# Projections as three one-pass products from stored high and low parts, and four maximum units moved between score blocks

## The chip, the cores and the metric

The kernel runs on one core of a Trainium2 chip. The metric is device time in microseconds (us) of one launch. The engines are TensorE (PE: matrix products; PEld: its weight loads), VectorE (DVE), ScalarE (ACT), GpSimd (POOL) and SyncE (SP), which here issues all transfers.

## The reference

Input x is 2 batches of 2048 rows of 256 numbers, float32. Attention with 16 heads of 64 runs on the normalised rows; then three blocks of a quantised two-layer network with low-rank terms follow.

```
keys    = einsum('bse,neh->bsnh', residual, W_key) + Bias_key      # queries, values alike
scores  = einsum('bknh,bqnh->bnqk', keys, queries) / sqrt(64)
scores  = where(q < k, 1e-10, scores)          # masked keys keep a weight
probs   = softmax(scores)
out     = einsum('bnqk,bknh->bqnh', probs, values) -> W_output + Bias_output
x = x + attention(layernorm(x));  x = x + ffn(layernorm(x))
```

The masked scores are not minus infinity, so every query also takes the sum of the values of all later keys, times exp(-maximum). The kernel therefore needs each row's maximum before its scores.

## The kernel before

Attention works on **pairs** of heads (8 per batch, 16 in all) and on **chunks** of 512 queries, taken in the order 3, 2, 1, 0. A pair has 20 **tiles** of four key blocks each; a tile is one turn of TensorE's loop: the two score blocks of the next tile (`scores`, n = 0 and 1), then the two halves of this tile's product with the values (`weighted`). While pair i does this, the preparation of pair i+1 is spread over it by tables of **slots**, six to a tile: slots 6t and 6t+1 come after the first score block, 6t+2 and 6t+3 after the second, 6t+4 and 6t+5 after each half of `weighted`. `between` issues what a slot holds.

Prepared in slots are:

- twelve **projection units** (`project`, slots 3, 5, 9, 11, ... 35): query, key and value of a chunk, each a 128x256 by 256x512 product in float32 from the normalised, turned x, which stays in SBUF (`xs`, a view of `home`). ScalarE rounds the result to the high part (`high`, L933) and copies that to bf16; VectorE takes the low part (`low`, L1071); a value unit has only VectorE's copy (L1066);
- forty **maximum units** (`max_unit`, table `MAX_AT`): for each head a bf16 product of 128 queries with up to 512 keys, whose maximum VectorE reads (`take_max`, L1085 and L1088);
- turned values, turned maxima and sums of probabilities (table `FIN`).

All of these write three background banks of PSUM in strict rotation: a projection takes one bank, a maximum unit two, one for each head. `bank_read` makes TensorE wait until the user three banks back has been read, so what sets the order around the change is these tables together with the rotation.

Scores are sums of one-pass products of high and low parts (float32r), 64 rows for each head, the heads side by side in the array; GpSimd adds up the probabilities (L669, L676), 18 of the 20 tiles of a pair. A row's maximum goes over DRAM to a row of SBUF (`keep_max`, `install_max`). SyncE issues everything in one written order and blocks on each wait. The second batch's x is normalised and turned while pair 6 runs. In the last pair VectorE does GpSimd's additions; then the weights of the network are turned, and the network runs as a block of its own.

Of the kernel before, what the change touches and what calls it, by code (L numbers as in the profile page):

```python
# [7 lines left out]
F32 = mybir.dt.float32  # L8
# [7 lines left out]
P = 128  # L16
CH = 512
# [70 lines left out]
PROJ_CHUNKS = [3, 2, 1, 0]  # L88
PROJ_SLOT = [6 * (u // 2) + (3, 5)[u % 2] for u in range(NPROJ)]
MAX_AT = [11, 15, 17, 21, 23, 27, 29, 33, 35, 37, 39, 41, 45, 47, 49, 51, 53, 57, 59, 61, 63, 65, 69, 71,  # L90
# [55 lines left out]
STATS_AT = {3: 50, 2: 56, 1: 78, 0: 84}  # L146
RSTD_TILE = {3: 10, 2: 11, 1: 14, 0: 15}
XN_AT = {3: 67, 2: 73, 1: 93, 0: 99}
TURN_AT = {3: 76, 2: 82, 1: 102, 0: 108}
# [43 lines left out]
def attention(nc, x, w_qkv, b_qkv, ffn_weights, max_kept, kept, inverses, ot, home):  # L193
# [14 lines left out]
    with ExitStack() as ctx:  # L208
# [11 lines left out]
        never_later = sb("never_later", [P, 2, 2, P], BF16)  # L220
        max_gate = sb("max_gate", [P, P], F32R)
        mask_q = sb("mask_q", [P, CH])
        ones64 = sb("ones64", [P, 64])
        ones_row = sb("ones_row", [P, CH], BF16)
# [3 lines left out]
        w_in = sb("w_in", [P, halves, 3, P])  # L228
        bias = sb("bias", [P, 3])
        xs = home.rearrange("p (c s t) -> p c s t", c=4, s=halves)  # L230
# [5 lines left out]
        rows = sb("rows", [40, 4, P], F32R)  # L236
# [15 lines left out]
        max_rows = sb("max_rows", [P, S], F32R)  # L252
        v = sb("v", [P, 16, P])
        v_from = sb("v_from", [P, 4, CH + 1])
# [5 lines left out]
        masked_num = sb("masked_num", [P, CH])  # L260
# [6 lines left out]
        chunk_rows = [xs[:, c].rearrange("p s (u d) -> p (s u) d", d=D) for c in range(4)]  # L267
# [6 lines left out]
        la_in = [xs[0:R, 3, l // 2, (l % 2) * D:(l % 2 + 1) * D] for l in range(4)]  # L274
# [5 lines left out]
        w_t = [xs[:, l // 2, l % 2, :] for l in range(n_layers)]  # L280
# [22 lines left out]
        xs_ready = sem("xs_ready")  # L303
        ffn_w_loaded = sem("ffn_w_loaded")
# [27 lines left out]
        row_kept = sem("row_kept")  # L332
        e_ready = sem("e_ready")
        e_kept = sem("e_kept")
# [31 lines left out]
        def ln_count(batch, c):  # L366
            return 4 * batch + PROJ_CHUNKS.index(c) + 1

        def xs_ready_count(batch, c):
            done = PROJ_CHUNKS.index(c) + 1  # L370
            return done if batch == 0 else 4 + 8 * (batch - 1) + 2 * done

# [4 lines left out]
        with nc.Block() as block:  # L377

            @block.sync
            def _(sp):  # L380
                def load_weights(j):

                    sp.wait_ge(proj_read, START + NPROJ * j)
                    pair = j % n_pairs
# [9 lines left out]
                def load_x(batch, c):  # L394

                    sp.wait_ge(proj_done, START + NPROJ * n_pairs * batch)
                    sp.dma_start(chunk_rows[c], x[4 * batch + c]).then_inc(xs_loaded[c], 16)

                def load_ffn_weights():

                    sp.wait_ge(proj_read, START + NPROJ * N)
                    sp.wait_ge(max_read, START + 2 * NMAX * N)
# [6 lines left out]
                    sp.dma_start(xs[0:R, 3].rearrange("r s (u d) -> r (s u) d", d=D),  # L409
                                 lora_a[0:4].rearrange("l r d -> r l d")).then_inc(ffn_w_loaded, 16)  # L410
# [5 lines left out]
                def keep_max(j, c):  # L416

                    sp.wait_ge(fin_read, START + reads("mt", j, c))
                    sp.dma_start(max_kept[j % 2, c], m_row[:, c, :].bitcast(F32)).then_inc(row_kept, 16)

                def install_max(j, c):

                    if j:
                        sp.wait_ge(pv_done, START + NT * (j - 1) + LAST_TILE[c] + 1)
                    sp.wait_ge(row_kept, START + 16 * (nth(j, c) + 1))
                    for h in range(2):
                        sp.dma_start(max_rows[64 * h:64 * h + 1, cols(c)].bitcast(F32),
                                     max_kept[j % 2, c, 4 * h:4 * h + 4].rearrange("r (o t) -> o (r t)", o=1)
                                     ).then_inc(row_in[c], 16)

                def keep_masked(j, c):

                    sp.wait_ge(e_ready, START + nth(j, c) + 1)
                    sp.dma_start(kept[j % 2, c], e8[:, c, :]).then_inc(e_kept, 16)

                def load_masked(i):

                    sp.wait_ge(e_kept, START + 64 * (i + 1))
# [55 lines left out]

                sp.wait_ge(consts, START + 2)
                load_weights(1)
                for k, (kind, c) in enumerate(FIN_FIRST):
                    if kind == "mt":
                        keep_max(0, c)
                        keep_masked(0, c)  # L500
                        install_max(0, c)
                for i in range(N):
                    more = i + 1 < N
                    if i:
                        spread_inverse(i - 1, 1)
                        take_den(i - 1, 0)
                        install_max(i, 0)
                        put_inverse(i - 1, 0)
                    load_masked(i)
                    spread_masked(i, 3)  # L510
                    if i:
                        spread_inverse(i - 1, 0)
                        store_heads(i - 1, 1)
                    spread_masked(i, 2)
                    if i:
# [3 lines left out]
                    if i + 2 < N:  # L519
                        load_weights(i + 2)  # L520
                        if (i + 2) % n_pairs == 0:
                            for c in PROJ_CHUNKS:
                                load_x((i + 2) // n_pairs, c)
                    spread_masked(i, 1)
                    masked_rows(i, 3)
                    take_den(i, 3)
# [5 lines left out]
                    if more:  # L532
                        install_max(i + 1, 3)
                    spread_masked(i, 0)
                    masked_rows(i, 2)
                    store_heads(i, 3)
# [4 lines left out]
                    if more:  # L541
                        install_max(i + 1, 2)
                    put_inverse(i, 2)
                    masked_rows(i, 1)
                    spread_inverse(i, 2)
# [6 lines left out]
                    if more:  # L552
                        install_max(i + 1, 1)
                    store_heads(i, 2)
                    if more:
                        keep_max(i + 1, 0)
                        keep_masked(i + 1, 0)
                spread_inverse(N - 1, 1)
# [10 lines left out]
            def _(pool):  # L569
# [17 lines left out]
                g.memset(never_later[:, :, :, :], 0.0).then_inc(zeroed, 1)  # L587
                pool.wait_ge(zeroed, START + 5)
                for tile in (ident, ident_bf):
# [3 lines left out]
                g.affine_select(out=never_later[:, :, :, :], in_=never_later[:, :, :, :], compare_op=ALU.is_ge, fill=NEVER,  # L593
                                base=0, pattern=[[-64, 2], [64, 2], [-1, P]], channel_multiplier=1).then_inc(shaped, 1)
# [14 lines left out]
                pool.wait_ge(gate_zeroed, START + 1)  # L609
                for c in PROJ_CHUNKS:  # L610
                    invert_root(0, c)
                pool.wait_ge(xn_done, START + len(PROJ_CHUNKS))
# [13 lines left out]
                def masked_part(i, group):  # L626
# [4 lines left out]
                    pool.wait_ge(num_ready, START + n)  # L631
                    g.tensor_tensor(masked_num[:, :], v_from[:, group, 1:CH + 1],
# [9 lines left out]

                for i in range(N - 1):
                    n = 0
                    for t in range(LAST_TILE[1] + 1):
# [4 lines left out]
                        if t == MASKED_DEN_TILE:  # L650
                            masked_denominators(i)
                        for c in (1, 0):
# [41 lines left out]
            def _(pe):  # L694
# [8 lines left out]
                def project(j, u):  # L703
                    c, m = PROJ_CHUNKS[u // 3], u % 3
                    if u == 0:
                        pe.wait_ge(w_loaded, START + 144 * (j + 1))
                    if m == 0:
                        pe.wait_ge(xs_ready, START + xs_ready_count(j // n_pairs, c))
                    bank_read("proj", j, u)
                    for s in range(halves):  # L710
# [991 lines left out]
```

## Time and profile before

| | us |
|---|---|
| median of 3 runs (2272.66 to 7177.97) | 2277.4 |
| profiled execution, its own time | 2273.86 |
| its span | 2272.0 |
| TensorE busy | 2176.1 |
| GpSimd busy | 1359.2 |
| VectorE busy | 1311.6 |
| ScalarE busy | 900.7 |

A busy sum is over the whole span; matmuls are pipelined, so their busy times overlap by some 0.17 us at a join, and a difference of starts tells better what one of them costs. The steady pairs run from about 98 to 1801 us, 113.33 us each (the first projection of one pair starts at 438.44, that of the next at 551.77 us); the last pair ends by about 1876, the attention block by about 1901 us.

### The profile page before, as it was taken

To read this page: it belongs to the slowest core of one execution; us is meant where nothing else is said; L and a number is where in the kernel's file an instruction comes from. 1 tells how busy PE (TensorE), PEld (TensorE's weight loads), DVE (VectorE), ACT (ScalarE), POOL (GpSimd) and SP (SyncE) were. 2 spreads that over 40 slices of the span, in tenths; PEclk is the share of its full clock that TensorE was granted. 3 is DMA by queue.
4 is the path that set the end of the run, shared out by engine and by line. 5 is a ranking of instruction groups with operands and counts; after the bars stand their busy time and mean duration, and the time that the engine had idled before them with its cause. 6 is when DMAs were issued, how large, how long until landed. Compare 5 with 4: busy or idle time off the path is not lost. (4 is left out here: it accounts for less than half of the span.)

```text
span 2272.0 us, 37164 instructions
## 1 busy us (share of the span) xinstructions
PE 2176.1 (96%) x13152; PEld 1138.1 (50%) x13152; DVE 1311.6 (58%) x3583; ACT 900.7 (40%) x1764; POOL 1359.2 (60%) x1212
## 2 busy tenths in 40 slices
PE   6999999999999999999999999999999997899987
PEld 2344444445454545454444454444444556777764
DVE  6755555555555566565656565555555661456655
ACT  2244444444444446444444444444444440110111
POOL 1277777777777777787878777878787611111110
PEclk9699999999999999999999999999999997999998
DMA  1001010101010111111111111111110124311100
GB/s 45 18 13 49 18 49 17 50 17 49 18 49 17 49 54 31 36 32 35 33 34 33 33 34 33 36 31 37 30 38 22 45 70 144 139 65 47 65 19 19
DMA packets 117205, 93.92 MB, mean 41 GB/s; under 512 B 67552, under 2 KB 84128, under 8 KB 117024
## 3 DMA queue, kind: packets, MB, share of 16 engines
q1 hardware_dynamic: 117024, 91.55, 13.2%
q8 instruction: 108, 1.77, 0.3%
q14 instruction: 73, 0.60, 0.1%
HBM read 69.21 MB, written 21.76 MB: 40 GB/s over the span
## 5 line engine op out<-in xcount | busy, mean ns | idle before, releaser
L676 POOL TENSOR_TENSOR acc<-acc,probs 128x512 f32<-128x512 f32 (+1 forms) x900 | 1007.8, 1157 | 282.3 <-ACT probs L1026 282.2
L1026 ACT ACTIVATE probs<-ps_s 128x512 f32<-128x512 f32 (+1 forms) x1152 | 579.1, 576 | 566.5 <-PE ps_s L831 394.4
L1088 DVE TENSOR_REDUCE partial<-ps_bg 128x1 f32<-128x512 f32 x768 | 486.9, 683 | 143.8 <-PE ps_bg L763 143.8
L853 PE MATMUL ps_o<-probs,v 128*64 128x512 f32 (+3 forms) x2560 | 538.1, 541 | 0.0
L711 PE MATMUL ps_bg<-home,w_in 128*128 128x512 f32 x768 | 381.9, 620 | 17.9 <-DVE q_lo L1071 10.6
L823 PE MATMUL ps_s<-q_hi,k_hi 64*128 64x512 f32 (+3 forms) x1280 | 299.7, 460 | 0.0
L763 PE MATMUL ps_bg<-k_bf,q_bf 64*128 64x512 bf16 (+3 forms) x1280 | 281.0, 361 | 16.0 <-DVE partial L1085 3.4
L853 PEld LDWEIGHTS ps_o<-probs,v 128*64 128x64 f32 x2560 | 155.3, 136 | 231.3 <-issue 184.1
L763 PEld LDWEIGHTS ps_bg<-k_bf,q_bf 64*128 64x128 bf16 x1280 | 78.0, 93 | 376.9 <-issue 333.1
L1085 DVE CUSTOM_DVE_ANT_0 junk<-ps_bg,mask_q 128x512 bf16<-128x512 f32 (+3 forms) x512 | 230.2, 484 | 41.2 <-issue 40.1
L829 PE MATMUL ps_s<-q_hi,k_lo 64*128 64x512 f32 (+3 forms) x1280 | 239.0, 362 | 0.0
L826 PE MATMUL ps_s<-q_lo,k_hi 64*128 64x512 f32 (+3 forms) x1280 | 238.9, 362 | 0.0
L831 PE MATMUL ps_s<-max_rows,max_gate 64*128 64x512 f32 (+3 forms) x1280 | 238.4, 361 | 0.0
L711 PEld LDWEIGHTS ps_bg<-home,w_in 128*128 128x128 f32 x768 | 130.7, 189 | 198.7 <-issue 153.6
L1417 POOL TENSOR_TENSOR c_rstd<-c_var,c_minus_half 128x4 f32<-128x4 f32 x32 | 35.5, 1110 | 275.7 <-DVE c_var L1592 275.7
L669 POOL TENSOR_TENSOR acc<-probs 128x512 f32<-128x512 f32 x90 | 114.0, 1290 | 116.0 <-ACT probs L1026 62.8
L1071 DVE SCALAR_TENSOR_TENSOR q_lo<-ps_bg,bias,q_hi 128x512 fp32r<-128x512 f32 x64 | 48.0, 751 | 214.4 <-ACT q_hi L933 214.4
L823 PEld LDWEIGHTS ps_s<-q_hi,k_hi 64*128 64x128 f32 x1280 | 126.3, 189 | 41.8 <-issue 26.9
L640 POOL TENSOR_TENSOR num<-num,scale 128x512 f32<-128x512 f32 x64 | 93.6, 1463 | 75.7 <-DMA scale<-inverse_sums 75.7
L831 PEld LDWEIGHTS ps_s<-max_rows,max_gate 64*128 64x128 f32 x1280 | 125.5, 185 | 17.7
L829 PEld LDWEIGHTS ps_s<-q_hi,k_lo 64*128 64x128 f32 x1280 | 125.4, 185 | 16.8
L826 PEld LDWEIGHTS ps_s<-q_lo,k_hi 64*128 64x128 f32 x1280 | 126.6, 187 | 9.7
(124 smaller groups left out, 2065.2 us busy)
## 6 DMA issues: line engine op xcount, KB each, us to landing
e<-masked_weights SPq DMA_DIRECT2D x128, 128.0 KB, 3.0
scale<-inverse_sums SPq DMA_DIRECT2D x128, 128.0 KB, 2.9
heads_turned<-num SPq DMA_DIRECT2D x64, 256.0 KB, 2.0
c_o_in<-heads_turned SPq DMA_DIRECT2D x6, 2048.0 KB, 7.7
home<-in_L_attn_residual SPq DMA_DIRECT2D x8, 512.0 KB, 5.2
c_o_in<-heads_turned SPq DMA_DIRECT2D x8, 512.0 KB, 8.5
c_x_in<-in_L_attn_residual SPq DMA_DIRECT2D x8, 512.0 KB, 8.2
out<-c_y SPq DMA_DIRECT2D x8, 512.0 KB, 2.8
```

Of the source, the lines that this page charges most:

```text
L669: g.tensor_tensor(acc[h][:, group % 2, :], pr[:, 0:CH], pr[:, CH:2 * CH], ALU.add).then_inc(added, 1)
L676: g.tensor_tensor(acc[h][:, group % 2, q0:q0 + w], acc[h][:, group % 2, q0:q0 + w], probs[h][:, probs_slot(i, t), at:at + w], ALU.add).the ...
L711: mm = pe.matmul(bank("proj", j, u), w_in[:, s, m, :], xs[:, c, s, :], start=(s == 0), stop=(s == halves - 1))
L763: pe.matmul(bank("max", j, n, h)[:, 0:w], q_bf[HEAD[h], qb * P:(qb + 1) * P], k_bf[HEAD[h], CH * u:CH * u + w], start=True, stop=True).the ...
L823: pe.matmul(out[h], k_hi[HEAD[h], i % 2, keys], q_hi[HEAD[h], i % 2, q], start=True, stop=False, skip_group_check=True)
L826: pe.matmul(out[h], k_hi[HEAD[h], i % 2, keys], q_lo[HEAD[h], i % 2, q], start=False, stop=False, skip_group_check=True)
L829: pe.matmul(out[h], k_lo[HEAD[h], i % 2, keys], q_hi[HEAD[h], i % 2, q], start=False, stop=False, skip_group_check=True)
L831: last = [pe.matmul(out[h], max_gate[HEAD[h], :], max_rows[HEAD[h], q], start=False, stop=not diagonal, skip_group_check=True) for h in ra ...
L853: mm = pe.matmul(ps_o[64 * h:64 * h + 64, q0:q0 + w], v[:, kb, 64 * h:64 * h + 64], probs[h][:, probs_slot(i, t), at:at + w], start=first, ...
L1026: nc.scalar.activation(probs[h][:, probs_slot(i, t), CH * half:end], ps_s[:, k % SCORE_BANKS, 0:end - CH * half], ACT.Exp, scale=SCORE_SCA ...
L1085: e.tensor_tensor_reduce(junk[:, k, 0:w], of, mask_q[:, CH - w:CH], 1.0, 3 * NEVER, ALU.add, ALU.max, to).then_inc(max_read, 1)
L1088: e.reduce_max(to, of, AX.X).then_inc(max_read, 1)
```

## The change

It does four things.

1. A projection unit is now six one-pass float32r products (high weights by high x, high weights by low x, low weights by high x, for each half of the 256) in place of two float32 ones. ScalarE rounds the weights to `w_hi` (`weights_high`, slot 64, or before the pairs begin), GpSimd takes `w_lo` (`weights_low`, ahead of tile 12's additions).
2. The high and low parts of x of a batch are formed once (ScalarE's copy, then VectorE's `x_low`), written to DRAM (`keep_x`), and brought back for each pair chunk by chunk into two buffers of 1 MB (`load_parts`).
3. To make room, buffers shrink or are shared: two slots of maximum rows in place of four (so `install_max` moves in SyncE's order), `masked_num` goes, the running sums of values lie in `home`, the mask is bf16, a row of ones becomes a column.
4. Four maximum units of a pair move from slots 15, 21, 27 and 33 (behind a projection) to 13, 19, 25 and 31 (between the two score blocks of that tile). The second batch's chunks are normalised in the order 1, 0, 3, 2.

```diff
-MAX_AT = [11, 15, 17, 21, 23, 27, 29, 33, 35, ...
+MAX_AT = [11, 13, 17, 19, 23, 25, 29, 31, 35, ...
+W_HIGH_AT = 64
+W_LOW_TILE = 12
...
+                def load_parts(j, k):
+                    sp.wait_ge(proj_done, START + (NPROJ * j + 3 * (k - 1) if k >= 2 else NPROJ * (j - 1) + 3 * (k + 3)))
+                    sp.wait_ge(x_out[k % 2], START + 32 * (j // n_pairs + 1))
+                    sp.dma_start(x_part[:, k % 2].bitcast(F32), x_kept[j // n_pairs, PROJ_CHUNKS[k]]
+                                 ).then_inc(x_in[k % 2], 16)
...
+                def weights_low(j):
+                    pool.wait_ge(w_high, START + j + 1)
+                    g.tensor_tensor(w_lo[:, :, :, :], w_in[:, :, :, :], w_hi[:, :, :, :].bitcast(F32), ALU.subtract
+                                    ).then_inc(w_ready, 1)
...
-                    for s in range(halves):
-                        mm = pe.matmul(bank("proj", j, u), w_in[:, s, m, :], xs[:, c, s, :],
-                                       start=(s == 0), stop=(s == halves - 1))
+                    products = [(w_of, z, s) for s in range(halves) for w_of, z in ((w_hi, 0), (w_hi, 1), (w_lo, 0))]
+                    for n, (w_of, z, s) in enumerate(products):
+                        mm = pe.matmul(bank("proj", j, u), w_of[:, s, m, :], x_part[:, k % 2, z, s, :],
+                                       start=(n == 0), stop=(n == len(products) - 1))
...
+                def x_low(batch, c):
+                    k = LN_CHUNKS[batch].index(c)
+                    for s in range(halves):
+                        dve.wait_ge(x_high, START + x_high_count(batch, c, s))
+                        low = e.tensor_tensor(x_part[:, k % 2, 1, s, :], turned(batch, c, s),
+                                              x_part[:, k % 2, 0, s, :].bitcast(F32), ALU.subtract)
```

On TensorE, around the first product of key positions of chunk 0 (tile 4 of a steady pair), `L711` is one projection unit, `L763` a maximum unit, `L823` to `L831` a score block and `L853` the product with the values. Before:

```order
L853 MATMUL ps_o<-probs,v 64x256 x2
L853 MATMUL ps_o<-probs,v 64x128 x2
L711 MATMUL ps_bg<-home,w_in 128x512 x2
L763 MATMUL ps_bg<-k_bf,q_bf 128x512 x2
L823 MATMUL ps_s<-q_hi,k_hi 128x512 x2
L826 MATMUL ps_s<-q_lo,k_hi 128x512 x2
L829 MATMUL ps_s<-q_hi,k_lo 128x512 x2
L831 MATMUL ps_s<-max_rows,max_gate 128x512 x2
```

and on to the second score block (the same four rows), then

```order
L711 MATMUL ps_bg<-home,w_in 128x512 x2
L763 MATMUL ps_bg<-k_bf,q_bf 128x512 x2
L853 MATMUL ps_o<-probs,v 64x512 x4
L711 MATMUL ps_bg<-home,w_in 128x512 x2
```

The same place of the changed kernel, from the projection unit on (`L797` is now the projection, `L850` the maximum unit, `L911` to `L919` a score block):

```order
L797 MATMUL ps_bg<-x_part,w_hi 128x512 x2
L797 MATMUL ps_bg<-x_part,w_lo 128x512
L850 MATMUL ps_bg<-k_bf,q_bf 128x512 x2
L911 MATMUL ps_s<-q_hi,k_hi 128x512 x2
L914 MATMUL ps_s<-q_lo,k_hi 128x512 x2
L917 MATMUL ps_s<-q_hi,k_lo 128x512 x2
L919 MATMUL ps_s<-max_rows,max_gate 128x512 x2
L850 MATMUL ps_bg<-k_bf,q_bf 128x512 x2
L911 MATMUL ps_s<-q_hi,k_hi 128x512 x2
```

The maximum unit that stood behind the next projection now stands one score block behind the last one.

On SyncE, in the first third of a steady pair, the loads of the parts of x stand among the small transfers (`e0` and `scale` are rows spread over 64 partitions, `heads_turned` the output of a head pair):

```order
L501 DMA e0<-masked_weights 64x512 x2
L440 DMA x_part<-high_and_low_x 128x2048
L533 DMA scale<-inverse_sums 64x512 x2
L539 DMA heads_turned<-num 128x512
L501 DMA e0<-masked_weights 64x512 x2
L440 DMA x_part<-high_and_low_x 128x2048
L539 DMA heads_turned<-num 128x512
L440 DMA x_part<-high_and_low_x 128x2048 x2
```

The `L440` rows are new; the others stood in this order before.

## Rows read from the trace of the kernel before

**Rows 1.** The page's first part: busy us, share of the span, instructions.

```profile
PE 2176.1 (96%) x13152; PEld 1138.1 (50%) x13152; DVE 1311.6 (58%) x3583; ACT 900.7 (40%) x1764; POOL 1359.2 (60%) x1212
```

**Rows 2.** Windows by stage: busy of PE, PEld, DVE, ACT, POOL, clock, DMA share, GB/s.

```profile
0.00:92.00 92.00, 65.12 (x176) 22.67 (x176) 67.61 (x218) 19.38 (x32) 8.01 (x23) 0.82 0.12 32
...
438.44:551.77 113.33, 111.84 (x726) 53.68 (x724) 65.01 (x179) 52.18 (x105) 85.56 (x76) 1.00 0.11 33
```

**Rows 3.** Groups of instructions by form: count, busy us, mean ns, idle before.

```profile
L711 PE MATMUL ps_bg<-home,w_in 128*128 128x512 f32 x768 | 381.9, 620 | 17.9 <-DVE q_lo L1071 10.6 <-DVE k_lo L1071 2.8 <-ACT home L976 1.2
...
L1506 PE MATMUL c_ps<-c_wo,c_o_in 128*128 128x256 f32 x128 | 30.1, 401 | 9.9 <-DMA c_o_in<-heads_turned 9.9
```

**Rows 4.** TensorE's timeline in one pair: start us, duration us, idle before.

```profile
446.62 1.98 PE L711 MATMUL ps_bg<-home,w_in 128*128 128x512 f32 x4
448.53 1.94 PE L853 MATMUL ps_o<-probs,v 128*64 128x512 f32 x8
...
452.31 0.39 PE L763 MATMUL ps_bg<-k_bf,q_bf 64*128 64x512 bf16 x2
...
453.08 0.30 PE L823 MATMUL ps_s<-q_hi,k_hi 64*128 64x128 f32 x2
...
461.76 1.98 PE L711 MATMUL ps_bg<-home,w_in 128*128 128x512 f32 x4
...
465.31 1.98 PE L711 MATMUL ps_bg<-home,w_in 128*128 128x512 f32 x4 [0.60 <-DVE q_lo L1071]
...
471.31 0.39 PE L763 MATMUL ps_bg<-k_bf,q_bf 64*128 64x512 bf16 x2
471.63 1.94 PE L853 MATMUL ps_o<-probs,v 128*64 128x512 f32 x8
...
475.42 0.39 PE L763 MATMUL ps_bg<-k_bf,q_bf 64*128 64x512 bf16 x2
...
476.56 0.39 PE L823 MATMUL ps_s<-q_hi,k_hi 64*128 64x512 f32 x2
...
481.67 1.98 PE L711 MATMUL ps_bg<-home,w_in 128*128 128x512 f32 x4
...
484.73 0.75 PE L763 MATMUL ps_bg<-k_bf,q_bf 64*128 64x512 bf16 x2
485.19 0.52 PE L823 MATMUL ps_s<-q_hi,k_hi 64*128 64x512 f32 x2
```

**Rows 5.** ScalarE's and VectorE's timelines beside Rows 4.

```profile
463.79 0.69 ACT L933 ACTIVATE q_hi<-ps_bg,bias 128x512 fp32r<-128x512 f32 x1 [0.69 <-PE ps_bg L711]
...
464.51 0.75 DVE L1071 SCALAR_TENSOR_TENSOR q_lo<-ps_bg,bias,q_hi 128x512 fp32r<-128x512 f32 x1 [3.24 <-ACT q_hi L933]
...
483.69 0.75 DVE L1066 TENSOR_SCALAR vt<-ps_bg,bias 128x512 f32<-128x512 f32 x1 [1.44 <-PE ps_bg L711]
484.35 3.67 DVE L1088 TENSOR_REDUCE partial<-ps_bg 128x1 f32<-128x512 f32 x6
```

**Rows 6.** GpSimd's and TensorE's timelines late in the same pair.

```profile
523.96 5.84 POOL L676 TENSOR_TENSOR acc<-acc,probs 128x512 f32<-128x512 f32 x4 [0.46 <-ACT probs L1026]
...
530.80 6.66 POOL L676 TENSOR_TENSOR acc<-acc,probs 128x512 f32<-128x512 f32 x8
...
539.42 1.08 PE L790 MATMUL ps_bg<-acc,ones 128*64 128x512 f32 x4
```

**Rows 7.** Issues of transfers (KB, us to landing), and one row of SyncE's timeline.

```profile
vt<-in_L_ffn_qweights SPq DMA_DIRECT2D x1, 1024.0 KB, 6.4
...
c_o_in<-heads_turned SPq DMA_DIRECT2D x8, 512.0 KB, 8.5
...
560.61 1.13 SPq L449 DMA_DIRECT2D e<-masked_weights  x2
```

**Rows 8.** TensorE's and VectorE's timelines at the start.

```profile
17.17 3.75 PE L711 MATMUL ps_bg<-home,w_in 128*128 128x512 f32 x4 [1.19 <-ACT home L976]
...
17.91 1.38 DVE L1209 TENSOR_SCALAR home<-home,mv,rstd 128x256 f32<-128x256 f32 x4 [1.13 <-POOL rstd L576]
```

More of the change, by code:

```diff
@@ L303, in attention @@
         xs_ready = sem("xs_ready")
+        x_high = sem("x_high")
+        x_out = [sem(f"x_out{b}") for b in range(2)]
+        x_in = [sem(f"x_in{b}") for b in range(2)]
+        w_high = sem("w_high")
+        w_ready = sem("w_ready")
+        la_loaded = sem("la_loaded")
         ffn_w_loaded = sem("ffn_w_loaded")
@@ L366, in ln_count, with turned, x_rows, kept_count @@
         def ln_count(batch, c):
-            return 4 * batch + PROJ_CHUNKS.index(c) + 1
+            return 4 * batch + LN_CHUNKS[batch].index(c) + 1
         def xs_ready_count(batch, c):
-            done = PROJ_CHUNKS.index(c) + 1
+            done = LN_CHUNKS[batch].index(c) + 1
             return done if batch == 0 else 4 + 8 * (batch - 1) + 2 * done
+        def turned(batch, c, s):
+            if batch:
+                return bank("ln", batch, c, s)
+            return ps_s[:, s] if ln_count(0, c) % 2 else (ps_s[:, 2], ps_o[:, :])[s]
+        def x_rows(batch, c):
+            k = LN_CHUNKS[batch].index(c)
+            return rows_at[k % 2 if batch else k]
+        def kept_count(j, c):
+            return 16 * (2 * j + (1 if c >= 2 else 2))
+        def x_slot(c):
+            return PROJ_CHUNKS.index(c) % 2
+        def x_high_count(batch, c, s):
+            return 8 * batch + 2 * LN_CHUNKS[batch].index(c) + s + 1
         def next_batch(i):
@@ L510, in _ @@
                     spread_masked(i, 3)
+                    if more:
+                        load_parts(i + 1, 2)
                     if i:
@@ L531, in _ @@
                         keep_masked(i + 1, 3)
-                    if more:
-                        install_max(i + 1, 3)
                     spread_masked(i, 0)
+                    install_max(i, 0)
                     masked_rows(i, 2)
+                    if next_batch(i) is not None:
+                        for c in LN_CHUNKS[next_batch(i)][2:4]:
+                            load_x(next_batch(i), c)
+                        for c in LN_CHUNKS[next_batch(i)][0:2]:
+                            keep_x(next_batch(i), c)
                     store_heads(i, 3)
@@ L557, in _ @@
                         keep_masked(i + 1, 0)
+                    if next_batch(i) is not None:
+                        for c in LN_CHUNKS[next_batch(i)][2:4]:
+                            keep_x(next_batch(i), c)
+                load_la()
                 spread_inverse(N - 1, 1)
@@ L651, in _ @@
                             masked_denominators(i)
+                        if t == W_LOW_TILE and i + 2 < N:
+                            weights_low(i + 2)
                         for c in (1, 0):
@@ L830, in scores @@
                                   skip_group_check=True)
-                    last = [pe.matmul(out[h], max_gate[HEAD[h], :], max_rows[HEAD[h], q], start=False,
+                    last = [pe.matmul(out[h], max_gate[HEAD[h], :], of_rows[HEAD[h], :], start=False,
                                       stop=not diagonal, skip_group_check=True) for h in range(2)]
@@ L1073, in low @@
                                            ).then_inc(proj_read, 1)
+                def x_low(batch, c):
+                    k = LN_CHUNKS[batch].index(c)
+                    for s in range(halves):
+                        dve.wait_ge(x_high, START + x_high_count(batch, c, s))
+                        low = e.tensor_tensor(x_part[:, k % 2, 1, s, :], turned(batch, c, s),
+                                              x_part[:, k % 2, 0, s, :].bitcast(F32), ALU.subtract)
+                        if batch or s == halves - 1:
+                            low.then_inc(xs_ready, 1)
                 def take_max(j, n):
```

204 lines of the change are left out of this document (124 added, 80 removed).

## The prediction, made before the changed kernel ran

> **What bounds the kernel.** I read the busy shares first, then the windows by stage, the timeline of one pair on TensorE, and beside it those of the engines that empty its banks. TensorE is busy 96% of the span, GpSimd 60%, VectorE 58% [rows 1]. In one steady pair TensorE is busy 111.84 of 113.33 us at the full granted clock, GpSimd 85.56 [rows 2], and the pairs repeat. So in the pairs TensorE's instruction stream is the time: what is taken out of it is gained, a stall put into it is lost, and the others matter only where TensorE waits for them. The start is different: TensorE 65 of 92 us, VectorE 68 [rows 2], a chain through both. Fifteen pairs have projections prepared in slots (180 units); the first pair's twelve belong to the start.
>
 The change makes it six single passes of 512 columns, each with its own weight load of 128 columns. No row shows this form. The nearest is the network's first product, whose records also carry 512 columns of work (2 x 256) with a weight load each: 30.1 us for 128 records, 0.235 each [rows 3]. I take that: 6 x 0.235 + 0.19 = **1.60 us**, a gain of 0.31. The other end is 0.215, what a pass costs inside today's unit (half of 0.43), with the weight loads wholly covered: 1.48 us, a gain of 0.43. Twelve units of a pair gain 3.72 us (5.16 at the other end).
>
> **The moved maximum units.** A unit behind a projection and ahead of `weighted` costs 471.63 - 471.31 = 0.32 us today [rows 4]. Between two score blocks it meets the bank rotation. Behind the tile's last projection P the banks go: P in b; the even maximum unit in b+1 and b+2; the moved odd unit in b and b+1. So its first head needs P read, its second needs the even unit's first head read. TensorE executes in order and stands still meanwhile.
>
> Today there is one such place, slot 37, and it checks the reasoning. P is a value unit from 481.67 to 483.65; VectorE's copy starts at 483.69, its first maximum at 484.35, and TensorE, which came to the unit at 484.73, goes on with the score block at 485.19 [rows 4, 5]. The chain from P's end is 0.04 + 0.66 + 0.84 = 1.54 us. For a query or key unit ScalarE comes in between: end of P at 461.76 + 1.98 = 463.74, ScalarE 463.79, VectorE 464.51 [rows 4, 5], so 0.05 + 0.72 + 0.66 + 0.84 = 2.27 us. (The 0.60 idle at 465.31 [rows 4] is this chain without the maximum.)
>
> With the new unit, P ends 0.11 (of the 0.19) + 5 x 0.235 + 0.39 (one pass of 512 to its end, as at 476.56 [rows 4]) = 1.68 us after its start. TensorE reaches the moved unit 1.60 us after that start plus the even unit and a score block, 476.56 - 475.42 = 1.14 us [rows 4]: at 2.74. It can go on at 1.68 + 2.27 = 3.95 behind a query or key unit: 1.21 us, less 0.32 in the old place, **0.89 more**. That is the case at slots 25 and 31. At 13 the block in front is 256 columns wide, 453.08 - 452.31 = 0.77 [rows 4], so TensorE comes at 2.37 and loses 1.58 - 0.32 = 1.26. At 19 P is a value unit: 1.68 + 1.54 - 2.74 - 0.32 = 0.16. Sum 3.20 us a pair. In return the 0.60 stall goes, as that projection now follows a half-tile later in the rotation; the rest of the queue is unchanged. What is late next is the projection behind the stalled block; its bank's last reader ends by 4.5 us after P's start (3.2 plus two reads of 0.61), and TensorE is there at 5.0, so it does not wait. Net 2.60 us a pair, so a pair gains 3.72 - 2.60 = 1.12, and fifteen **16.8 us**. With new units but the old table a pair would gain 3.7.
>
> **Work put on the others.** `weights_low` is one instruction of 768 columns on GpSimd, ahead of tile 12's additions. At 5.84 / 4 = 1.46 us for 512 [rows 6] it takes 2.2 us. From there GpSimd has 0.46 us of idle, and its last addition ends at 537.46, 1.96 us before TensorE needs it at 539.42 [rows 6]: 2.42 of cover, so nothing. If that cover is gone the sums' product waits: at 3.0 us, 0.6 a pair, 9 in all. ScalarE's rounding of the weights (at most 1.5 x 0.69) lies in an engine busy 52 of 113 us. The maximum row of the next pair's first tile is installed later, but still three tiles ahead of the scores that need it: nothing, against a load of 2 KB.
>
> **The parts of x.** Four transfers of 1 MB a pair. Two have most of a pair's time. The third is issued when the first chunk's units are done and SyncE is past the `e` transfers, 560.61 + 1.13 = 561.74, 10.0 us after the pair's start at 551.77 [rows 7]; at 6.4 us for 1 MB [rows 7] it lands at 16.7, and its chunk is needed where now 461.76 - 438.44 = 23.3 us stands [rows 4], about 22 with shorter units: 5 us spare. The fourth has two tiles (481.67 - 465.31 = 16.4) less a unit, some 13.5 us, between the buffer's last reader and its first user. Small transfers queued behind them go up to 6 us later; the one for GpSimd at tile 4 meets an engine that idles a quarter of the pair. Cost nothing; upper bound below.
>
> **Once only.** Start: the first projection must wait for VectorE's two subtractions, which stand behind the second chunk's normalisation, 17.91 + 1.38 = 19.3, plus 1.4: 20.7 in place of 17.17 [rows 8], +3.5; six more subtractions of 0.7 on the same chain, +4.2, less 0.31 for some nine units in it, -2.8: **+5** (bounds -3 if the chain has slack, +9). Second batch: eight subtractions between the turned banks and their next users, **+3** (0 to 6). End: the first low-rank input is loaded behind the last masked product, **+1** (-1 to a whole load, 6).
>
> **Sum.** 2273.9 (the profiled execution) - 16.8 + 5 + 3 + 1 = **2266 us**. The median of the runs shown is 3.5 higher; I leave that inside the range.
>
> **Rivals.**
> *A pass at 0.215 us.* Today's own unit does run at that pace; against it stands the network's record at 0.235. Then the pair gains 5.16 - 2.60 = 2.56, fifteen 38.4: 2273.9 - 38.4 + 9 = **2244**. The Trainium skill says this on "TensorE: Matmul & The Clock Gate", section "Wait — 56ns, not 53.3ns?": a warm matmul starts every N / 2.4 GHz + 2.5 ns, 215.7 ns at 512 columns. It agrees with the passes inside `L711`, not with `L1506`; by that rule the sum comes out as this rival's.
> *The stalls don't arise*, because ScalarE and VectorE are through sooner than the chain says. For it: busy 46% and 57% of a pair. Against: slot 37 behaves to 0.02 us as computed. The pair then gains 3.72 + 0.60 = 4.32: 2273.9 - 64.8 + 9 = **2218**.
> *The parts of x come late* (the side of slower). A row shows 512 KB taking 8.5 us in a crowded queue [rows 7]; 1 MB at that pace takes 17, the third transfer lands 5 us late and the fourth 4, 9 us a pair, 135 in all: **2400**. It decides once a landing takes over 12 us; about 12.5 makes the kernel slower than before. Against it: DMA share 0.11 in the pair [rows 2], and long runs of memory.
>
> **Chances.** Forecast 0.58, the faster pass 0.20, no stalls 0.12, late parts 0.10. 2% of 2277 is 45 us, about what can be told from no change. Faster by over 2% is below 2232: the no-stall rival and some of the fast pass with smaller stalls, 0.17. Slower by over 2% is above 2323: 0.08 of the late parts. Within 2%: 0.75. The forecast's own range is 2250 to 2290 (+9 GpSimd, +4 start, +3 batch, +3.5 median; -16 for stalls half as long). The full range takes in the two faster rivals: 2215 to 2290.
>
> **What would show it.** Six records in a projection, starts 0.235 apart, slot 1.60 us. In tiles 2, 4 and 5 a `ps_bg` maximum unit between score blocks with 1.2 to 1.6 us from its start to the next block, its releaser VectorE's maximum; tile 3 next to nothing. Pair length 112.2 us. No wait for `x_part` but at the start, none of the sums' product for GpSimd over 0.2. Wrong if a pair is below 110 (stalls absent, or passes of 0.215) or TensorE waits for a transfer in the pairs.

## The result, and the profile after

| | before | after |
|---|---|---|
| median, both on one chip | 2275.03 us (4 runs) | 2391.78 us (4 runs) |
| ratio | | 1.0516, interval 1.0474 to 1.0559 |
| span of the profiled execution | 2272.0 | 2394.6 |

The change makes the kernel 5.2% slower, by 117 us; 2266 was predicted, with 2290 as the upper end. The ratio compares fast executions alone, so it leaves out the one of 7177.97 us before. The page's first part after (as rows 1):

```profile
PE 2178.1 (91%) x13536; PEld 1245.1 (52%) x13536; DVE 1420.0 (59%) x3599; ACT 919.0 (38%) x1782; POOL 1369.5 (57%) x1228
```

TensorE is busy as long as before [rows 1], so, on balance, nearly all of the 122 us of span are waits. VectorE has 108 us more busy time for 16 more instructions: some instruction there has become long. The groups by line name it (busy us, mean ns); of before, then of after:

```profile
L1101 DVE TENSOR_TENSOR_SCAN v_from<-ones_row,v_from,vt 128x512 f32<-128x512 bf16 x64 | 85.4, 1334 | 1.7
```

```profile
L1211 DVE TENSOR_TENSOR_SCAN home<-one_col,home,vt 128x512 f32<-128x512 f32 x64 | 184.6, 2884 | 1.7
```

This is `scan`, the running sum of the values over the keys, four for each pair. Of all its executions after (shortest, median and longest in ns):

```profile
L1211 DVE TENSOR_TENSOR_SCAN home<-one_col,home,vt x64: 1273/1285/8557, 100.9 to 1920.4; 128x512 f32<-128x512 f32 x64
```

The median is unchanged; thirteen scans, all at slot 86 (tile 14, the values of chunk 2), take 8.50 to 8.56 us. Slot 86 is reached in fifteen pairs, 0 to 14. The two short ones are in pair 6, which also normalises the second batch (GpSimd idles from 921.95 us on, and the scan starts at 923.78), and in pair 14, the one pair of them in which no `weights_low` is taken, since no pair after the next is left to prepare. There the idle time is open, and the scan is short, inside the changed kernel itself (GpSimd, then VectorE):

```profile
1892.56 5.84 POOL L758 TENSOR_TENSOR acc<-acc,probs 128x512 f32<-128x512 f32 x4 [0.50 <-ACT probs L1124]
```

```profile
1892.34 1.28 DVE L1211 TENSOR_TENSOR_SCAN home<-one_col,home,vt 128x512 f32<-128x512 f32 x1
```

TensorE's waits say who pays (us in total, times, longest):

```profile
PE ps_bg L850 <- DVE partial L1195: 92.4, 35, 6.7
...
PE ps_bg L850 <- DVE q_lo L1171: 18.0, 30, 0.8
...
PE ps_bg L850 <- DVE k_lo L1171: 6.7, 16, 0.5
...
PE ps_bg L797 <- DVE x_part L1180: 3.7, 1, 3.7
```

`L1195` is VectorE's read of a maximum. One such wait on VectorE's, GpSimd's and TensorE's timelines, in the pair whose first projection starts at 470.62:

```profile
554.69 8.53 DVE L1211 TENSOR_TENSOR_SCAN home<-one_col,home,vt 128x512 f32<-128x512 f32 x1
563.16 0.41 DVE L1195 CUSTOM_DVE_ANT_0 junk<-ps_bg,mask_q 128x256 bf16<-128x256 f32 x1
```

```profile
544.10 1.80 POOL L683 TENSOR_TENSOR w_lo<-w_in,w_hi 128x768 fp32r<-128x768 f32 x1
545.88 4.42 POOL L758 TENSOR_TENSOR acc<-acc,probs 128x512 f32<-128x512 f32 x4
550.26 1.27 POOL L719 TENSOR_TENSOR num<-num,scale 128x512 f32<-128x512 f32 x1
551.50 2.26 POOL L758 TENSOR_TENSOR acc<-acc,probs 128x256 f32<-128x256 f32 x4
553.72 2.49 POOL L751 TENSOR_TENSOR acc<-probs 128x512 f32<-128x512 f32 x2
556.18 4.91 POOL L758 TENSOR_TENSOR acc<-acc,probs 128x512 f32<-128x512 f32 x4
561.06 1.08 POOL L711 TENSOR_TENSOR num<-home,e 128x512 f32<-128x512 f32 x1
568.24 6.61 POOL L758 TENSOR_TENSOR acc<-acc,probs 128x512 f32<-128x512 f32 x8 [6.09 <-ACT probs L1124]
```

```profile
556.73 0.23 PE L850 MATMUL ps_bg<-k_bf,q_bf 64*128 64x128 bf16 x1
563.64 0.28 PE L850 MATMUL ps_bg<-k_bf,q_bf 64*128 64x128 bf16 x1 [6.68 <-DVE partial L1195]
563.74 0.80 PE L911 MATMUL ps_s<-q_hi,k_hi 64*128 64x512 f32 x2
```

The scan's record ends at 563.22, one scan's length of 1.28 behind 561.94, and that is where GpSimd's run of instructions ends, but for 0.2 us (its last record ends at 562.14; the same 0.2 stands between them in the long scans of experiment 2). Before, the `[0.46 <-ACT probs L1026]` of [rows 6] stood at this place: GpSimd idle from 523.50 to 523.96, and in it the scan:

```profile
523.74 1.28 DVE L1101 TENSOR_TENSOR_SCAN v_from<-ones_row,v_from,vt 128x512 f32<-128x512 bf16 x1
```

Now `weights_low` has used that gap up, GpSimd goes from one instruction to the next from 544.10 to 562.14, and the scan, ready in the middle of the pair of `L751`, stands through the rest of that instruction and six more. Behind it stand VectorE's maxima, behind them TensorE. GpSimd's run ends there because it has nothing left to add: its next addition comes after 6.09 us of idle, and waits for ScalarE's `probs`, made from scores that TensorE computes only when it goes on at 563.74. Then comes a second price. Windows of the changed kernel (us, busy of PE, PEld, DVE, ACT, POOL, granted clock, DMA share, GB/s): a pair, and the 5 us behind the wait.

```profile
470.62:591.10 120.48, 111.00 (x750) 59.92 (x748) 72.58 (x179) 53.31 (x106) 85.40 (x77) 0.97 0.21 66
...
563.60:568.60 5.00, 4.96 (x33) 3.27 (x35) 1.87 (x10) 1.96 (x4) 0.36 (x1) 0.68 0.00 0
```

After 6.7 us of standing still TensorE's granted clock is at its lower level, 1.2 GHz, until about 567: two score blocks take 567.09 - 563.74 = 3.35 us where the same at 574.16 take 2.04.

### The profile page after: what moved, and what is told of

Read it like the earlier page. It is cut to its first block and busy times, and to the rows that moved or that the text cites. A ratio compares the mean times of both kernels' runs of the same rounds, so it can differ in the third digit from the quotient of the medians.

```text
span 2394.6 us, 38162 instructions
## 1 busy us (share of the span) xinstructions
PE 2178.1 (91%) x13536; PEld 1245.1 (52%) x13536; DVE 1420.0 (59%) x3599; ACT 919.0 (38%) x1782; POOL 1369.5 (57%) x1228
## 5 line engine op out<-in xcount | busy, mean ns | idle before, releaser
L850 PE MATMUL ps_bg<-k_bf,q_bf 64*128 64x512 bf16 (+3 forms) x1280 | 305.5, 364 | 137.7 <-DVE partial L1195 92.4
L850 PEld LDWEIGHTS ps_bg<-k_bf,q_bf 64*128 64x128 bf16 x1280 | 85.3, 94 | 455.7 <-issue 261.9
L911 PE MATMUL ps_s<-q_hi,k_hi 64*128 64x512 f32 (+3 forms) x1280 | 314.4, 479 | 0.0
L797 PE MATMUL ps_bg<-x_part,w_hi 128*128 128x512 f32 x768 | 263.1, 424 | 10.2 <-DVE x_part L1180 3.7
L1195 DVE CUSTOM_DVE_ANT_0 junk<-ps_bg,mask_q 128x512 bf16<-128x512 f32 (+3 forms) x512 | 227.3, 484 | 37.6 <-issue 36.5
L917 PE MATMUL ps_s<-q_hi,k_lo 64*128 64x512 f32 (+3 forms) x1280 | 248.3, 371 | 0.0
L914 PE MATMUL ps_s<-q_lo,k_hi 64*128 64x512 f32 (+3 forms) x1280 | 248.0, 370 | 0.0
L919 PE MATMUL ps_s<-max_rows,max_gate 64*128 64x512 f32 (+3 forms) x1280 | 247.9, 370 | 0.0
L797 PEld LDWEIGHTS ps_bg<-x_part,w_hi 128*128 128x128 f32 x768 | 130.8, 190 | 114.1 <-issue 76.1
L719 POOL TENSOR_TENSOR num<-num,scale 128x512 f32<-128x512 f32 x64 | 84.0, 1313 | 184.7 <-DMA scale<-inverse_sums 184.7
L1211 DVE TENSOR_TENSOR_SCAN home<-one_col,home,vt 128x512 f32<-128x512 f32 x64 | 184.6, 2884 | 1.7
L797 PE MATMUL ps_bg<-x_part,w_lo 128*128 128x512 f32 x384 | 152.3, 397 | 0.0
L911 PEld LDWEIGHTS ps_s<-q_hi,k_hi 64*128 64x128 f32 x1280 | 131.6, 194 | 33.4 <-issue 20.4
L751 POOL TENSOR_TENSOR acc<-probs 128x512 f32<-128x512 f32 x90 | 115.0, 1303 | 58.4 <-PE ps_bg L883 57.6
L919 PEld LDWEIGHTS ps_s<-max_rows,max_gate 64*128 64x128 f32 x1280 | 133.3, 191 | 15.8
```

The lines of the kernel that those rows point to most:

```text
L797: mm = pe.matmul(bank("proj", j, u), w_of[:, s, m, :], x_part[:, k % 2, z, s, :], start=(n == 0), stop=(n == len(products) - 1))
L850: pe.matmul(bank("max", j, n, h)[:, 0:w], q_bf[HEAD[h], qb * P:(qb + 1) * P], k_bf[HEAD[h], CH * u:CH * u + w], start=True, stop=True).the ...
L911: pe.matmul(out[h], k_hi[HEAD[h], i % 2, keys], q_hi[HEAD[h], i % 2, q], start=True, stop=False, skip_group_check=True)
L914: pe.matmul(out[h], k_hi[HEAD[h], i % 2, keys], q_lo[HEAD[h], i % 2, q], start=False, stop=False, skip_group_check=True)
L917: pe.matmul(out[h], k_lo[HEAD[h], i % 2, keys], q_hi[HEAD[h], i % 2, q], start=False, stop=False, skip_group_check=True)
L919: last = [pe.matmul(out[h], max_gate[HEAD[h], :], of_rows[HEAD[h], :], start=False, stop=not diagonal, skip_group_check=True) for h in ran ...
```

## Theories

A: `weights_low` closes the gap in GpSimd's additions, and the scan, which needs an opening there, waits for the whole run. B: the scan's changed first operand (a float32 column, broadcast, for a bf16 row) makes it slow. C: the new transfers disturb it. The price of the moved maximum units is a question of its own, tested beside these.

## The experiments

**1. Move `weights_low` to the end of the pair**, where GpSimd idles.

```diff
-                        if t == W_LOW_TILE and i + 2 < N:
-                            weights_low(i + 2)
...
                     masked_part(i, 0)
+                    if i + 2 < N:
+                        weights_low(i + 2)
                     normalise(i, 2)
```

> Changed kernel, with the low part of the weights taken by GpSimd at the end of its pair, ahead of the third chunk's normalisation, in place of ahead of tile 12's additions; nothing else differs. Theory A (its place closes the 0.46 us gap in GpSimd's additions in which VectorE's scan of the values of chunk 2 began, and the scan then waits for six GpSimd instructions): the scan at slot 86 falls from 8.5 to 1.3-1.8 us, the 6.68 us wait of TensorE behind it goes, pairs of about 112.5 us in place of 121.3, time 2391.8 - 13 x 9.2 = 2272 us (2265 to 2280). Theory B (the scan's changed operands, a float32 column of ones broadcast in place of a bf16 row, are what slows it): scan stays 8.5, 2390. Theory C (the transfers of the parts of x disturb SBUF): scan stays long, 2385 to 2392.

Measured: 2268.3 us (10 runs; before beside it 2274.08), ratio 0.9974 (0.9955 to 0.9993). One instruction of each pair, moved, takes 123.5 us off. Its gap and scan, and the window of one pair:

```profile
522.91 2.52 POOL L749 TENSOR_TENSOR acc<-probs 128x512 f32<-128x512 f32 x2
525.91 5.83 POOL L756 TENSOR_TENSOR acc<-acc,probs 128x512 f32<-128x512 f32 x4 [0.48 <-ACT probs L1124]
```

```profile
525.68 1.28 DVE L1211 TENSOR_TENSOR_SCAN home<-one_col,home,vt 128x512 f32<-128x512 f32 x1
```

```profile
441.60:553.71 112.11, 109.30 (x750) 58.62 (x748) 65.46 (x179) 53.24 (x106) 86.32 (x77) 1.00 0.23 71
```

A pair lasts 112.11 us; 112.2 was predicted for the change. B and C fall: scan form and transfers are all there.

**2. The kernel before with only 1.5 us more on GpSimd.**

```diff
+                        if t == 12 and i + 2 < N:
+                            pool.wait_ge(dosed, START + i + 1)
+                            g.tensor_tensor(dose[:, 0], dose[:, 1], dose[:, 1], ALU.mult).then_inc(dosed, 1)
```

> Kernel before, plus one unused product of 128x768 float32 on GpSimd ahead of tile 12's additions in the pairs 0 to 13 (extra work whose output nobody reads). Nothing else of the change. Theory A: that alone makes the scan at slot 86 take 8.5 us in about 13 pairs, TensorE waits 6.7 us behind it, pairs 113.3 -> about 122, time 2275 + 13 x 9 = 2390 us (2370 to 2400). Theories B and C: the extra 1.8 us is hidden, 2275 us and scans of 1.3.

Measured: 2394.54 us, ratio 1.0528 (1.0502 to 1.0555). One instruction a pair (14 in all) whose result nobody reads costs 120 us in a kernel with none of the change. Thirteen scans of 8.19 to 8.27 us; GpSimd, VectorE and TensorE in one pair:

```profile
661.79 1.46 POOL L653 TENSOR_TENSOR dose<-dose 128x768 f32<-128x768 f32 x1
...
671.10 2.50 POOL L676 TENSOR_TENSOR acc<-probs 128x512 f32<-128x512 f32 x2
673.56 4.92 POOL L683 TENSOR_TENSOR acc<-acc,probs 128x512 f32<-128x512 f32 x4
678.45 1.08 POOL L634 TENSOR_TENSOR masked_num<-v_from,e 128x512 f32<-128x512 f32 x1
```

```profile
672.35 8.27 DVE L1108 TENSOR_TENSOR_SCAN v_from<-ones_row,v_from,vt 128x512 f32<-128x512 bf16 x1
```

```profile
681.02 0.28 PE L770 MATMUL ps_bg<-k_bf,q_bf 64*128 64x128 bf16 x1 [6.41 <-DVE partial L1092]
```

**3. The kernel before with the changed operand of the scan.**

```diff
-    e.tensor_tensor_scan(out=..., data0=ones_row[:, :],
+    e.tensor_tensor_scan(out=..., data0=one_col[:, 0:1].to_broadcast([P, CH]),
```

> Kernel before, with the scan's first operand a float32 column of ones broadcast to 512 columns, as in the changed kernel, in place of a bf16 row. Theory A: scans 1.3-1.8 us, 2275 us (2270 to 2280). Theory B: the scan at slot 86 takes 8.5 us and the time is about 2390.

Measured: 2279.52 us, ratio 1.0008 (0.9986 to 1.003), the longest scan 1.78 us. B is refuted directly.

**4. The same extra instruction, smaller**, 32, 128 and 256 columns, one execution each.

> Kernel before with an unused GpSimd product of 128x32, in the place where the 128x768 one stood. By the additions (0.56 us for 256 columns, 1.25 for 512) about 0.15 us, which leaves 0.3 of the 0.46 us gap. Theory A: nothing lost, 2275 us, scans of 1.3 us. If any GpSimd instruction there were enough: 2390.

> The same with 128x128, about 0.35 us, which leaves 0.1 us of the gap. Theory A expects an on/off outcome pair by pair: either the scan slips into what is left of the gap (scan below 1.6 us, pair 113.3) or it waits for all six instructions (about 8.3 us, pair 122), and a whole time between 2275 and 2395 only as a count of pairs of the two sorts. A cost that grows with the dose (the scan waiting only for the added instruction) would show scans of 1.5 us and 2275 to 2280.

> Kernel before with an unused GpSimd product of 128x256 ahead of tile 12's additions: by the rows of the smaller doses (0.27 us for 32 columns, 0.39 for 128) and 0.56 for 256 about 0.6 us, more than the 0.46 us gap. Theory A: the switch lies between 128 and 256 columns: scan of about 8.3 us in about 13 pairs, 2390 us. A cost that grows with the dose: scan 1.5 us, about 2270 us.

| columns | its time | GpSimd idle ahead of tile 15 | scans over 3 us | time |
|---|---|---|---|---|
| 0 (the profiled execution) | - | 0.46 | 0 | 2273.86 |
| 32 | 0.27 | 0.25 | 0 | 2266.54 |
| 128 | 0.39 | 0.10 | 0 | 2267.27 |
| 256 | 0.62 | none | 2 | 2283.82 |
| 768 | 1.46 | none | 13 | 2394.54 |

The outcome is on/off pair by pair, no cost grows with the dose; but the switch is not where I put it, between 128 and 256 columns. It lies between 0.62 and 1.46 us of extra work. At 256 columns the gap is gone and still only two scans are long; the time is two pairs' worth, 2 x 8.2 = 16 us above the smaller doses. GpSimd and VectorE in a pair where the scan got in, then in one where it didn't:

```profile
409.30 1.28 POOL L676 TENSOR_TENSOR acc<-probs 128x512 f32<-128x512 f32 x1
410.53 5.91 POOL L683 TENSOR_TENSOR acc<-acc,probs 128x512 f32<-128x512 f32 x4
...
521.38 2.54 POOL L676 TENSOR_TENSOR acc<-probs 128x512 f32<-128x512 f32 x2
523.85 4.96 POOL L683 TENSOR_TENSOR acc<-acc,probs 128x512 f32<-128x512 f32 x4
```

```profile
410.22 1.45 DVE L1108 TENSOR_TENSOR_SCAN v_from<-ones_row,v_from,vt 128x512 f32<-128x512 bf16 x1
```

```profile
523.55 7.39 DVE L1108 TENSOR_TENSOR_SCAN v_from<-ones_row,v_from,vt 128x512 f32<-128x512 bf16 x1
```

The two engines exclude each other, and the loser waits: 5.91 - 4.96 = 0.95 us when GpSimd loses, 7.39 - 1.28 = 6.11 when the scan does. In both pairs the scan came 0.37 us ahead of the end of `L676`. What decides in this case I can't say.

So theory A is too strong where it says that the scan needs an opening. The kernel before shows that too, in the scan of the values of chunk 0, at slot 3 of each pair, which comes in the middle of four additions in a row (GpSimd, then VectorE):

```profile
553.18 5.89 POOL L676 TENSOR_TENSOR acc<-acc,probs 128x512 f32<-128x512 f32 x4 [0.69 <-ACT probs L1026]
```

```profile
555.36 1.41 DVE L1101 TENSOR_TENSOR_SCAN v_from<-ones_row,v_from,vt 128x512 f32<-128x512 bf16 x1
```

It gets in as soon as the addition under way ends, 0.33 us later, and it is GpSimd that loses 0.9 us. That holds in pairs 0 to 14 of every trace, the changed kernel's too (1.41 to 1.76 us there): 210 scans, ready 0.19 to 1.15 us ahead of the boundary at which they got in. At slot 86, 78 scans of all traces came while GpSimd went from one instruction to the next, and 67 of them missed the next boundary: 52 came 0.27 to 0.31 us ahead of it (the thirteen of the changed kernel among them), 13 came 1.17 to 1.25 ahead (768 columns), two 0.37. The 11 that got in came 0.31 to 0.37 ahead. So the moment of arrival alone does not decide; what sets slot 86 apart, and why a scan that misses one boundary misses the next ones too, stays open. Shown is what `weights_low` did at this slot.

**5. Make GpSimd wait for the scan.** The changed kernel with `weights_low` where the change put it, and a wait added ahead of one tile's additions.

```diff
+                        if t == FIRST_TILE[1] + 1:
+                            pool.wait_ge(sums_ready, START + 4 * (i + 1) + 2)
```

A first version had `FIRST_TILE[0]`, which puts the wait at tile 19, where GpSimd's loop (tiles 0 to 17) does not come. Its expectation was

> Changed kernel with only a wait added: GpSimd does not begin the additions of the tile behind group 0's first until VectorE's scan of the values of chunk 2 has ended. Nothing is moved or removed. Theory A (a scan that is ready finds GpSimd's instructions back to back and waits for all of them): the scan starts when the first tile's additions end, takes 1.3-1.8 us, GpSimd idles about 1.5 us there and is about 0.8 us late for the sums' product of chunk 1, 12 us in all: 2272 + 12 = 2284 us (2268 to 2295), although work is only delayed. Theory B (form of the scan) or C (the transfers): the scan still takes 8.5 us, GpSimd is 8 us late besides, 2391 us or more.

and it measured 2390.61 us with 13 long scans: the changed kernel once more, and no test of anything. The second:

> The run before it with this wait put it behind group 0's first tile, which GpSimd's loop does not reach, so nothing waited: it repeats the changed kernel (2390.6 us). Here GpSimd waits for the scan of the values of chunk 2 ahead of the additions of tile 15, the tile behind group 1's first; nothing else differs from the changed kernel. Theory A: scan 1.3-1.8 us, GpSimd idles some 1.5 us there and is up to 0.8 us late for the sums' product of chunk 1: 2268 to 2284 us. Theory B or C: scan 8.5 us, GpSimd 8 us late besides: 2391 us or more.

Measured: 2277.94 us (10 runs), ratio to before 1.0019 (1.0 to 1.0038). A wait alone, with no work taken away, makes the changed kernel 114 us faster. GpSimd, then VectorE:

```profile
529.25 2.54 POOL L753 TENSOR_TENSOR acc<-probs 128x512 f32<-128x512 f32 x2
532.96 4.98 POOL L760 TENSOR_TENSOR acc<-acc,probs 128x512 f32<-128x512 f32 x4 [1.16 <-DVE home L1213]
```

```profile
530.29 2.59 DVE L1213 TENSOR_TENSOR_SCAN home<-one_col,home,vt 128x512 f32<-128x512 f32 x1
```

The scan comes at 530.29, during the first of the two `L753`; it still waits through the second, to 531.79, and then has its time, again but for 0.2 us. At this place a scan that came while GpSimd worked got in, here and in the changed kernel, only where GpSimd's run ended, and to end the run is enough to bring it in.

**6. The moved maximum units**, three ways: back to their old slots with `weights_low` late, back with it in place, and the move alone in the kernel before.

```diff
-MAX_AT = [11, 13, 17, 19, 23, 25, 29, 31, 35,
+MAX_AT = [11, 15, 17, 21, 23, 27, 29, 33, 35,
```

> As the run with the low part of the weights late, and the four moved maximum units back in their old slots 15, 21, 27, 33. The term of the prediction says that the move costs 2.60 us a pair: 15 x 2.6 = 39 us less than that run, about 2233 us. Rival (the stalls at the moved units are paid for elsewhere, the same chain then delays the next projection): less than 10 us of difference.

> Changed kernel with the four moved maximum units back in slots 15, 21, 27, 33; the low part of the weights stays ahead of tile 12. If the two costs add: 2391.8 - 39 = 2353 us (2345 to 2360), scans of 8.5 us. If the moved units were needed for the long scan (they shift VectorE against GpSimd): about 2235 us.

> Kernel before with only the four maximum units moved to slots 13, 19, 25, 31. By the prediction's term 2.60 us a pair: 2275 + 39 = 2314 us (2305 to 2322), scans of 1.3 us. Rival (the old projection leaves other times in the rotation, or the stalls are given back later): below 2290.

| | with the move | without | difference |
|---|---|---|---|
| `weights_low` late | 2268.3 | 2234.39 | 33.9 |
| as changed | 2391.78 | 2350.14 | 41.6 |
| kernel before | 2308.7 | 2272.93 | 35.8 |

Ratios to before: 0.9817 (0.9799 to 0.9834), 1.0326 (1.03 to 1.0353) and 1.0145 (1.0122 to 1.0168). One pair of the first and of the last of these kernels:

```profile
435.25:544.59 109.34, 107.94 (x750) 58.11 (x749) 65.43 (x179) 52.90 (x106) 86.33 (x77) 1.00 0.24 71
```

```profile
446.84:562.87 116.03, 113.19 (x726) 54.05 (x724) 65.01 (x179) 52.49 (x105) 85.22 (x76) 1.00 0.12 34
```

The move costs 112.11 - 109.34 = 2.77 us a pair with the new units and 116.03 - 113.33 = 2.70 with the old; 2.60 was computed. Over the whole kernel 39 us were said, and 34 to 42 measured. The costs add: the long scans are there with either table.

**7. The version to keep.** As the first kernel of 6, with three more units away from a score block and the start's low parts earlier.

```diff
-... 35, 37, 39, 41, 45,
+... 35, 39, 41, 43, 45,
...
-                for c in (3, 2):
-                    row_stats(0, c)
-                    standardise(c)
+                row_stats(0, 3)
+                standardise(3)
+                row_stats(0, 2)
+                x_low(0, 3)
+                standardise(2)
```

> The run with the low part of the weights late and the old maximum table (2234 us), with two more moves: maximum units 37, 39, 41 to slots 39, 41, 43, away from the score block behind the last projection (TensorE stands 0.46 us there), and at the start VectorE's two low parts of x of chunk 3 ahead of the normalisation of chunk 2. By the rotation: 15 x 0.2 to 0.45 = 3 to 7 us, and 1 to 1.5 us at the start: 2234 - 6 = 2228 us (2224 to 2236). Rival: the units bunched at 39 to 45 meet a chain of maxima behind each other and cost what they gain: 2233.

Measured: 2224.43 us (6 runs), ratio 0.9789 (0.9764 to 0.9815): 2.1% faster than before, 7% faster than the change as made, and inside the 2224 to 2236 that were expected. A pair lasts 109.05 us, 0.3 less than in the first kernel of 6; that is some 4 us, and the first pair starts 2.1 us sooner. The rest of the 10 us between the two medians is within the spread of these six runs, 2216.57 to 2231.91.

## Why the prediction was wrong, point by point

- **The projection unit: the size right, its source misread.** 1.60 us computed; measured 476.10 - 474.51 = 1.59, its records 0.23 apart:

```profile
474.51 0.73 PE L797 MATMUL ps_bg<-x_part,w_hi 128*128 128x512 f32 x2
475.08 0.39 PE L797 MATMUL ps_bg<-x_part,w_lo 128*128 128x512 f32 x1
475.31 0.62 PE L797 MATMUL ps_bg<-x_part,w_hi 128*128 128x512 f32 x2
475.77 0.40 PE L797 MATMUL ps_bg<-x_part,w_lo 128*128 128x512 f32 x1
476.10 0.49 PE L911 MATMUL ps_s<-q_hi,k_hi 64*128 64x512 f32 x2
```

  With the old table a pair went from 113.33 to 109.34: 3.99, where 3.72 was the sum. But the 0.235 it was worked out from is a mean over two levels of the clock. The first eleven of the 128 records of `L1506` ran at a granted clock of 0.51; at 1.00 the window's 112 take 23.93 us, some 0.215 each (windows of `L1506` before: us, busy of PE and PEld, clock, DMA share, GB/s):

```profile
1911.05:1915.75 4.70, 4.70 (x11) 3.80 (x12) 0.51 1.03 380
1916.87:1940.80 23.93, 23.93 (x112) 21.09 (x111) 1.00 0.79 261
```

  So this row spoke for the rival of 0.215 and not against it, and that the forecast came out at 0.23 was luck in this term. The row to use was a score product of before, a one-pass product of 512 columns with its own weight load (two heads side by side): three in a row start at 476.11, 476.34 and 476.56, 0.23 apart. The changed unit's records start 0.23 apart too, so the rival of 0.215 a pass does not hold for them, and nor does the Trainium skill's 215.7 ns at 512 columns ("TensorE: Matmul & The Clock Gate", section "Wait — 56ns, not 53.3ns?"). The records of `L1506` and the half records of `L711`, 0.215 each, agree with the skill's figure.
- **The moved maximum units: right.** 2.60 computed, 2.70 to 2.77 measured, and by the chain named. Slot 25: TensorE comes at about 498.63, waits for `k_lo`, goes on at 499.82, 1.19 us later (1.21 computed). The rival without stalls is refuted. Start by start, between before and the move alone in experiment 6, slots 13, 19, 25 and 31 cost 1.09, 0.27, 0.98 and 1.01 us (1.26, 0.16, 0.89 and 0.89 said), and the stall that goes gives back 0.67 (0.60 said). Slot 37 was no check of the chain, though: the 0.84 us in it were read from slot 37 itself.

```profile
498.40 0.40 PE L919 MATMUL ps_s<-max_rows,max_gate 64*128 64x512 f32 x2
499.21 0.90 PE L850 MATMUL ps_bg<-k_bf,q_bf 64*128 64x512 bf16 x2 [0.41 <-DVE k_lo L1171]
499.82 0.52 PE L911 MATMUL ps_s<-q_hi,k_hi 64*128 64x512 f32 x2
```

- **The parts of x: right.** The third load is issued 480.26 - 470.62 = 9.6 us behind the pair's start (10.0 said) and such a load lands 5.0 us later in the median (6.4 said). TensorE waits for no such transfer; the rival of late parts, my only one on the slower side, did not happen.

```profile
x_part<-high_and_low_x SPq DMA_DIRECT2D x58, 1024.0 KB, 5.0
```

- **Start and second batch: the sums near, the start's parts not.** The first pair's start moves by 5.8 us in experiment 1 (98.50 to 104.31; 5 said) and by 7.3 in the changed kernel itself. But the first projection alone moves from 17.17 to 23.62, 6.4 where 3.5 were said, and the rest, said to cost 1.4 more, gives 0.6 back in experiment 1: the two errors offset each other. In experiment 1 pair 6 is longer than its neighbours by 122.28 - 112.07 = 10.2, before by 7.1: 3.1 (3 said). The term for the end can't be read: from the start of pair 14 to the end it takes 571 to 586 us over these kernels, and two executions that differ only in the operand of the scan are 7 us apart there.
- **`weights_low`: the step that failed.** "From there GpSimd has 0.46 us of idle, and its last addition ends 1.96 us before TensorE needs it: 2.42 of cover, so nothing." Its length was 1.80 us, 2.2 said (the 5.84 us for four additions in [rows 6] hold a loss to the scan; four without one take 4.96) and TensorE indeed waits only once for GpSimd's sums, 2.1 us. I had asked who waits for GpSimd's results, not who works while GpSimd is idle. VectorE's scan began in the 0.46 us, and with `weights_low` in front of them it came into GpSimd's run and waited to its end. That cost per pair: 6.68 of wait, 3.35 - 2.04 = 1.31 at the lower clock, in sum 8.0 of the 120.48 - 112.11 = 8.4 by which the pair is longer than in experiment 1. In the pairs of 121.6 us the clock stays down longer: in the one from 591.10 on it is 0.52 from 684.20 to 690.00.

The rows to see it by were in the trace of before: the scan beginning at 523.74, in an idle time of GpSimd from 523.50 to 523.96, and the slower scans elsewhere, up to 2.25 us, where the two engines met. The Trainium skill has the rule ("SBUF — State Buffer", section "SBUF: two separate sides"): a VectorE operation with two inputs in SBUF and a GpSimd operation that reads SBUF lock a shared pair of ports, and the one that comes second is fully blocked for the other's whole instruction. The runs agree that they exclude each other. Read as it stands it would make the scan wait for one GpSimd instruction, at most 1.25 us. So it is with the scan at slot 3; at slot 86 it waited through seven in a row, and the rule as stated does not tell the two apart. Among VectorE's work in a steady pair the scan alone suffers: in the same run of GpSimd the reads of a maximum, whose one input is in PSUM, keep their 0.55 us for 384 columns.

Without this step the sum of the prediction stood: experiment 1 is the change with that one instruction elsewhere, and measured 2268.3 against 2266, 5.8 us below the kernel before beside it, where 7.9 were said.

## What to carry to other kernels

Before filling an idle time of GpSimd, look at what VectorE runs in it: if that has both inputs in SBUF, as the scan here, the idle time is in use, and its loss can cost a wait for the whole back-to-back run on GpSimd, many times the length of the added instruction. It does not always (the scan at slot 3, and most pairs at 256 columns), and these runs give no rule for when, so read the lengths of that instruction in the new trace. Put such work where GpSimd idles long, or make GpSimd wait at the one place. And a queue's "cover" has two sides, those who wait for its results and those who share something with it.

## What was not expected of the hardware

- A scan that is ready during a run of back-to-back GpSimd instructions waited for seven of them, 7.2 us, or only for the one under way, 0.1 to 0.5 us: in the changed kernel the scan at slot 86 did the first in thirteen pairs, and the scan at slot 3 the second in all of fifteen. With 256 columns added slot 86 did the second in 11 of 13 pairs.
- Opposite sizes of the two losses at slot 86: 0.95 us for GpSimd, 6.1 to 7.2 for VectorE.
- The cost is not in proportion to the added work: an extra instruction of 0.39 us a pair costs nothing, one of 0.62 us 17 us in all, one of 1.46 us 120 us.
